# Normalizations merged into the stages that read them, in a six-layer fp32 kernel on one Trainium2 core

## The reference

```python
x = x + 0.5 * moe(_layernorm(x))        # router, 64 experts of 64, the best 8 of each token, a shared expert
x = x + heads(_layernorm(x))            # 16 heads of 8, softmax attention
x = x + 0.5 * moe(_layernorm(x))
x = x + 0.5 * cell(_layernorm(x))       # recurrent: 4 steps (the batch axis), each over all 1024 tokens
x = x + decayed_attention(_layernorm(x))  # its own layernorm, attention, x2; then x2 + mlp(layernorm(x2))
x = x + 0.5 * cell(_layernorm(x))

def _layernorm(x, axis=-1, eps=1e-05):
    m = jnp.mean(x, axis=axis, keepdims=True)
    v = jnp.var(x, axis=axis, keepdims=True)
    return (x - m) / jnp.sqrt(v + eps)
```

## Time and profile before

| | |
|---|---|
| median of 3 runs | 2742.0 us (2739.37 to 2742.69) |
| the profiled execution: time | 2743.51 us |
| the profiled execution: span, first to last instruction | 2741.4 us |
| TensorE busy | 93% |
| VectorE busy | 81% |
| ScalarE busy | 66% |
| GpSimd busy | 45% |
| TensorE's mean granted clock | 0.966 of 2.4 GHz |

### The profile page before, as it was taken

One profiled execution on the slowest core, in us unless ns is written; L12 is line 12 of the kernel. 1 busy time (PEld: TensorE's weight loads), 2 busy tenths in 40 slices (PEclk: granted clock), 3 DMA queues, 4 the chain that ended last, 5 costly groups with the idle time before them and its releaser, 6 DMA issues. The chain is left out here.

```text
span 2741.4 us, 35099 instructions
## 1 busy us (share of the span) xinstructions
PE 2545.0 (93%) x11075; PEld 1905.2 (69%) x11075; DVE 2223.1 (81%) x3277; ACT 1821.2 (66%) x3026; POOL 1231.3 (45%) x1265
## 2 busy tenths in 40 slices
PE   6899999996999999999999997899999998788778
PEld 3688888874666666666666664688888885476556
DVE  6778777776999999999999996777787775567655
ACT  3455555556888888888888884455555555557665
POOL 3466666664323232332323322466666662245401
PEclk9999999998999999999999999999999999888999
DMA  3566666644333333333333321566666640100000
GB/s 85 118 138 145 145 142 135 136 103 164 98 107 99 106 102 97 109 100 104 104 103 101 98 93 34 127 144 138 135 146 145 143 105 8 32 16 8 8 8 31
DMA packets 107385, 271.47 MB, mean 99 GB/s; under 512 B 30784, under 2 KB 35648, under 8 KB 107072
## 3 DMA queue, kind: packets, MB, share of 16 engines
q1 hardware_dynamic: 82192, 235.42, 34.7%
q0 software_dynamic: 24576, 33.62, 4.4%
q10 hardware_dynamic: 432, 0.20, 0.0%
HBM read 258.35 MB, written 10.76 MB: 98 GB/s over the span
## 5 line engine op out<-in xcount | busy, mean ns | idle before, releaser
L614 POOL TENSOR_TENSOR moe_experts_lo<-moe_experts_hidden,moe_experts_hi 128x512 fp32r<-128x512 f32 x512 | 661.1, 1291 | 340.6 <-ACT moe_experts_hi L552 340.4
L895 DVE TENSOR_TENSOR heads_e_lo<-heads_e,heads_e_hi 128x1024 fp32r<-128x1024 f32 x512 | 616.1, 1224 | 25.7
L559 ACT ACTIVATE psum<-psum 128x512 f32<-128x512 f32 x512 | 298.0, 582 | 479.8 <-PE psum L90 479.8
L729 POOL DMA_DIRECT2D heads_left<-heads_parts x512 | 306.5, 612 | 671.3 <-PE psum L783 610.7
L835 ACT ACTIVATE heads_e<-psum 128x1024 f32<-128x1024 f32 x512 | 520.0, 1023 | 108.2 <-PE psum L783 108.2
L586 DVE TENSOR_TENSOR moe_experts_weighted<-moe_spread,psum 128x512 f32<-128x512 f32 x512 | 350.8, 685 | 190.2 <-PE psum L90 186.4
L88 PE MATMUL psum<-heads_e_hi,heads_v_lo 128*128 128x512 f32 x1024 | 429.4, 419 | 18.0 <-DVE heads_u L861 18.0
L88 PE MATMUL psum<-moe_n_hi,moe_w_lo 128*128 128x512 f32 x1024 | 400.8, 391 | 4.2 <-PEq L54 3.9
L89 PE MATMUL psum<-heads_e_lo,heads_v_hi 128*128 128x512 f32 x1024 | 404.2, 395 | 0.0
L90 PE MATMUL psum<-heads_e_hi,heads_v_hi 128*128 128x512 f32 x1024 | 400.9, 391 | 0.0
L89 PE MATMUL psum<-moe_n_lo,moe_w_hi 128*128 128x512 f32 x1024 | 400.2, 391 | 0.0
(11 more groups left out here) (403 smaller groups left out, 4093.8 us busy)
## 6 DMA issues: line engine op xcount, KB each, us to landing
moe_spread<-moe_mask SPq DMA_DIRECT2D x128, 1024.0 KB, 9.8
heads_right<-heads_parts SPq DMA_DIRECT2D x512, 64.0 KB
heads_left<-heads_parts POOLq DMA_DIRECT2D x512, 64.0 KB, 2.5
heads_scale<-heads_inverse_copy SPq DMA_DIRECT2D x64, 512.0 KB, 3.7
moe_experts_raw<-in_gate SPq DMA_DIRECT2D x16, 256.0 KB, 11.7
moe_experts_raw<-in_up SPq DMA_DIRECT2D x16, 256.0 KB, 11.8
moe_experts_raw<-in_down SPq DMA_DIRECT2D x16, 256.0 KB, 11.6
heads_parts<-heads_e_hi SPq DMA_DIRECT2D x16, 256.0 KB, 3.2
```

What stands on the lines that cost most here:

```text
L559: act.activation(psum[:, GATE + p % 2, :], psum[:, GATE + p % 2, :], ACT.Silu).then_inc(silu_ready, 1)
L614: pool.tensor_tensor(lo[:, p, :], hidden[:, p % 2, :], f(hi[:, p, :]), ALU.subtract).then_inc(low_ready, 1)
L729: eng.dma_start(f(tile[row:row + 2 * HEAD, h % 2, :]), parts_dram[dims, order:order + 2, at]).then_inc(loaded[h % 2], 16)
L895: dve.tensor_tensor(e_lo[:, s, :], e[:, s % 4, :], f(e_hi[:, s, :]), ALU.subtract).then_inc(low, 1)
```

## The change

`layernorm` becomes a class `Norm`, whose methods give each engine's part, so that a stage can begin with a normalization and go on with its own work without a barrier. The stages of routing (twice), the cells (twice) and the MLP do so; the heads and the decayed attention keep a stage of their own. In detail:

- The stages wait for chunks instead of the barrier: `wait_low` for a chunk's low part (and with it the high part), `wait_weights` for the early splits, `wait_banks` for all scaled chunks and logarithms, which frees PSUM.
- The variances take two banks (4 and 5) instead of four. The low part of chunk 0 is VectorE's, in all seven.
- The splits of the first experts' weights come behind GpSimd's low parts (`late_splits`).
- Routing: the gate and up products of chunk 0 (`shared(0, 0)`) come right behind `logits(0, 0)`, ahead of the first turn.
- Cells: other banks for the sums (`SUMS`, `OUT`); the high part of the initial cell state is made by VectorE, and the initial state comes ahead of the normalization on its list.
- MLP: the banks of `up` and `down` are permuted so that `up(0, 0)` takes banks 4 to 7.

```diff
+class Norm:
     CENTERED, VARIANCE = 0, 4
-    BANKS = 4
-    RING = 4
-    SCALES = 3
-    VECTOR_LOWS = (2, 5, 7)
+    CENTERS, VARIANCES = 4, 2
+    RING, SCALES = 4, 3
+    VECTOR_LOWS = (0, 2, 5, 7)
...
+    def wait_low(self, eng, c):
+        who = "vector" if c in self.VECTOR_LOWS else "pool"
+        eng.wait_ge(self.low_ready[who], sum((i in self.VECTOR_LOWS) == (c in self.VECTOR_LOWS) for i in range(c + 1)))
+
+    def wait_weights(self, eng, count=None):
+        eng.wait_ge(self.split_low, self.early if count is None else count)
+
+    def wait_banks(self, eng):
+        eng.wait_ge(self.scaled_ready, CHUNKS)
+        eng.wait_ge(self.logs_taken, CHUNKS)
...
+        def variance(c):
+            pe.wait_ge(self.squares_ready, c + 1)
+            after(pe, self.logs_taken, c - self.VARIANCES + 1)
+            pe.matmul(self.psum[:, self.VARIANCE + c % self.VARIANCES, :], self.consts["inv"], self.squares[:, c % 3, :],
+                      start=True, stop=True).then_inc(self.variance_ready, 1)
...
+    def gpsimd(self, pool):
...
+        for i in range(self.early):
+            split(i)
+        for c in range(CHUNKS):
+            if c not in self.VECTOR_LOWS:
+                self.take_low(pool, "pool", c)
+        for i in range(self.early, len(self.splits)):
+            split(i)
...
@@ route_and_share, tensor
                 def logits(c, j):
+                    norm.wait_low(pe, c)
                     after(pe, affinity_ready, c)
...
+                def shared(c, j):
+                    after(pe, added, c - 1)
+                    product(pe, psum[:, GATE + j, :], gate, (n_hi[:, tokens(c)], n_lo[:, tokens(c)]))
+                    product(pe, psum[:, UP + j, :], up, (n_hi[:, tokens(c)], n_lo[:, tokens(c)])).then_inc(up_ready, 1)
+
                 def step(c, j, last):
                     if not last:
                         logits(c + 1, 1 - j)
-                    after(pe, added, c - 1)
-                    product(pe, psum[:, GATE + j, :], gate, (n_hi[:, tokens(c)], n_lo[:, tokens(c)]))
-                    product(pe, psum[:, UP + j, :], up, (n_hi[:, tokens(c)], n_lo[:, tokens(c)])).then_inc(up_ready, 1)
+                    if c > 0:
+                        shared(c, j)
...
+                norm.tensor(pe)
+                norm.wait_weights(pe)
+                pe.wait_ge(norm.scaled_ready, LOGITS + 5)
                 logits(0, 0)
+                pe.wait_ge(norm.log_ready, CHUNKS)
+                shared(0, 0)
+                norm.wait_banks(pe)
                 turn_affinity(0, 0)
...
@@ scalar, vector, gpsimd: each begins with its part of the normalization
+                norm.scalar(act)
                 affinities(0, 0)
...
+                norm.vector(dve)
                 each_chunk(step)
...
+                norm.gpsimd(pool)
                 each_chunk(step)
...
@@ moe_layer
-            layernorm(nc, f"{tag}_norm", psum, consts, x, n_hi[:, :], n_lo[:, :], splits=splits + first_group,
-                      x_dram=x_dram)
+            def normalization(sb, sem):
+                return Norm(sb, sem, f"{tag}_norm", psum, consts, x, n_hi[:, :], n_lo[:, :], splits=splits,
+                            late_splits=first_group, x_dram=x_dram)
...
@@ recurrent_layer
-        OUT = 6
+        start_high = sem("start_high")
+        SUMS = ((6, 7, 4), (5, 0, 1))
+        OUT = 2
...
                 def from_input(t):
                     for half in range(HALVES):
                         at = ds(t * T + half * BANK, BANK)
+                        norm.wait_low(pe, t * HALVES + half)
                         after(pe, gates_ready, t * (3 * HALVES) + (half - 1) * 3)
...
+                norm.tensor(pe)
+                norm.wait_weights(pe)
+                norm.wait_banks(pe)
                 from_input(0)
...
-                act.wait_ge(cell_ready, HALVES)
-                for half in range(HALVES):
-                    act.copy(c_hi[:, half, :], cell[:, half, :]).then_inc(high_ready, 1)
+                norm.scalar(act)
...
                 for half in range(HALVES):
-                    dve.wait_ge(high_ready, half + 1)
+                    dve.wait_ge(cell_ready, half + 1)
+                    dve.tensor_copy(c_hi[:, half, :], cell[:, half, :]).then_inc(start_high, 1)
+                for half in range(HALVES):
+                    dve.wait_ge(start_high, half + 1)
                     dve.tensor_tensor(c_lo[:, half, :], cell[:, half, :], f(c_hi[:, half, :]), ALU.subtract).then_inc(low_ready, 1)
+                norm.vector(dve)
...
@@ mlp_layer
+        def bank(j, m):
+            return psum[:, (1 - j) * W + (m + 2) % W, :]
...
                 def up(c, j):
+                    norm.wait_low(pe, c)
                     after(pe, y_ready, c - 1)
...
+                norm.tensor(pe)
+                norm.wait_weights(pe)
+                pe.wait_ge(norm.log_ready, CHUNKS)
                 up(0, 0)
+                norm.wait_banks(pe)
                 each_chunk(step)
```

More of the change, by code:

```diff
@@ new lines, in take_low, with sync @@
+    def take_low(self, eng, who, c):
+        eng.wait_ge(self.high_ready, c + 1)
+        eng.tensor_tensor(self.n_lo[:, self.chunk(c)], self.normal[:, c % self.RING, :], f(self.n_hi[:, self.chunk(c)]),
+                          ALU.subtract).then_inc(self.low_ready[who], 1)
+    def sync(self, sp):
+        for c, arrived in enumerate(self.x_loaded):
+            sp.dma_start(self.x[:, self.chunk(c)], self.x_dram[:, self.chunk(c)]).then_inc(arrived, 16)
+        for raw, (source, _, _), arrived in zip(self.raws, self.splits, self.raw_loaded):
+            sp.dma_start(raw[:, :], source).then_inc(arrived, 16)
+        for tile, source in self.loads:
+            sp.dma_start(tile, source).then_inc(self.tiles_loaded, 16)
+        if self.copies is not None:
+            for c in range(CHUNKS):
+                self.wait_low(sp, c)
+                for to, part in self.copies:
+                    sp.dma_start(to[:, self.chunk(c)], f((self.n_hi, self.n_lo)[part][:, self.chunk(c)])
+                                 ).then_inc(self.copied[c // HALVES], 16)
+        if self.loads:
+            sp.wait_ge(self.tiles_loaded, 16 * len(self.loads))
@@ new lines, in tensor, with difference @@
+    def tensor(self, pe):
+        def difference(c):
+            if self.x_loaded:
+                pe.wait_ge(self.x_loaded[c], 16)
+            after(pe, self.scaled_ready, c - self.CENTERS + 1)
+            pe.matmul(self.psum[:, self.CENTERED + c % self.CENTERS, :], self.consts["center"], self.x[:, self.chunk(c)],
+                      start=True, stop=True).then_inc(self.difference_ready, 1)
+        def variance(c):
[3 more added lines that the diff above has]
+                      start=True, stop=True).then_inc(self.variance_ready, 1)
+        for c in range(CHUNKS + 1):
+            if c < CHUNKS:
+                difference(c)
+            if c >= 1:
+                variance(c - 1)
@@ new lines, in vector, with scaled, high @@
+    def vector(self, dve):
+        def scaled(c):
+            to, centered = self.normal[:, c % self.RING, :], self.psum[:, self.CENTERED + c % self.CENTERS, :]
+            scale = self.scales[:, c % self.SCALES, :]
+            if c >= self.RING:
+                self.wait_low(dve, c - self.RING)
+            dve.wait_ge(self.scale_ready, c + 1)
+            if self.keep is not None:
+                dve.tensor_tensor(self.keep[:, self.chunk(c)], scale, centered, ALU.mult).then_inc(self.kept_ready, 1)
+                scale = self.both_scales[:, c % self.SCALES, :]
+                dve.wait_ge(self.both_scale_ready, c + 1)
+            dve.tensor_tensor(to, scale, centered, ALU.mult).then_inc(self.scaled_ready, 1)
+            if self.affine is not None:
+                dve.wait_ge(self.scaled_ready, c + 1)
+                dve.tensor_scalar(to, to, self.affine[0], self.affine[1], ALU.mult, ALU.add).then_inc(self.normal_ready, 1)
+        def high(c):
+            dve.wait_ge(self.normal_ready, c + 1)
+            dve.tensor_copy(self.n_hi[:, self.chunk(c)], self.normal[:, c % self.RING, :]).then_inc(self.high_ready, 1)
+        for c in range(CHUNKS + 1):
+            if c < CHUNKS:
+                scaled(c)
+                high(c)
+            if c - 1 in self.VECTOR_LOWS:
+                self.take_low(dve, "vector", c - 1)
+        if self.keep is not None:
+            dve.wait_ge(self.kept_ready, CHUNKS)
@@ L201, in variance @@
-                def variance(c):
-                    pe.wait_ge(squares_ready, c + 1)
-                    after(pe, log_ready if keep is None else both_log_ready, c - BANKS + 1)
-                    pe.matmul(psum[:, VARIANCE + c % BANKS, :], inv, squares[:, c % 3, :], start=True,
-                              stop=True).then_inc(variance_ready, 1)
-                for c in range(CHUNKS + 1):
-                    if c < CHUNKS:
-                        difference(c)
-                    if c >= 1:
```

(2 more changed lines are left out.)

226 lines of the change are left out of this document (103 added, 123 removed).

## The result

| | before | after |
|---|---|---|
| median | 2742.35 us (2739.37 to 2743.34, 4 runs) | 2723.82 us (2723.05 to 2725.68, 4 runs) |
| ratio, 95% interval | | 0.9935 (0.9918 to 0.9952) |
| profiled execution, span | 2741.4 us | 2721.8 us |

The kernel became 18.5 us faster. The prediction was 25.3 us: the sign was right, the size 7 us too large. The prediction's 2716.7 us missed by 7.1 us: the measured median lies 0.2 us inside the range of 2710 to 2724, and 0.8 us above the 2711 to 2723 of rival (a), to which I gave 0.78.

What follows compares the result with a forecast made beforehand. TensorE, busy 93% of 2741.4 us, bounds the kernel, so only its idle gaps can yield. 8.05 + 7.61 - 2.0 + 4.68 + 7.1 - 0.1 = 25.3 us takes the median from 2742.0 to 2716.7; range 2710 to 2724.

Steps and rivals of the forecast that it cites:

- rival (a): Whole kernel: the gain comes as summed, with a time of 2711 to 2723 us; chance 0.78.
- `pick(0)` 3.2 us after the last scale: MoE routing: `pick(0)` follows ScalarE's last scale by about 3.2 us, 6.86 us earlier in the first layer, 6.42 in the second.
- The wait of 1.19 before the first silu: MoE routing: VectorE's idle for `share` before `silu(0)` goes; bounds 0 and 1.19 us, taken in full in each layer.
- The port waits: MoE layers: `pick(0)`'s scalings wait for GpSimd's late splits; bounds 0 and 2.1 us, 1.0 taken per layer, 2.0 together.
- From `silu(0)` on the stage lasts as long as VectorE's list: MoE routing: what arrives earlier at `silu(0)` arrives earlier at the end; gains of 8.05 and 7.61 us.
- The table: MoE layers: ScalarE's Sigmoid table load takes 1.28 us with no drain showing; by the skill page, 1.4 us less won.
- The cells: Both recurrent cells: input products start 2.34 us earlier, TensorE's idle falls from 5.48 to 3.1 us; 4.68 us together.
- "pass on": Cells: the recurrence is a chain and hands on the full 2.34 us; no gain given for the clock.
- rival (b): Whole kernel: cells restart at full clock and splits collide with nothing, 2711.9 us or less; chance 0.08 of below 2711.
- The MLP: MLP stage: the first `y` comes at 2611.5 instead of 2618.59, 7.1 us earlier; 0.8 less if TensorE stays slow.
- the two paths that nearly coincided: MLP, to the first `y`: VectorE's path ends at 2611.4, TensorE's at 2611.5.
- The rest at zero: Other stretches: experts stay at 529 us, later MLP chunks repeat, decay's normalization loses nothing, heads lose 0.1 us.

Runs made afterwards that it cites:

- the run with the constants alone: Against the kernel before, only low part 0 on VectorE and variances in two banks, all stages separate as before: 2738.16 us, ratio 0.9990.

## Why the prediction was 7 us too large

Term by term, from the table of stretches and from the one counted from the first scaled chunk:

- **`pick(0)` 3.2 us after the last scale: right.** ScalarE's last scale ends at 26.99, `pick(0)` starts at 29.90, 2.91 later. From the first scaled chunk it comes 7.14 and 6.71 us earlier, where 6.86 and 6.42 were summed (7.27 and 5.66 by the second traces: in the kernel before, the second layer's normalization differs by 1 us between its two). VectorE's end of the normalization and the turned affinities nearly coincide, as forecast.
- **The wait of 1.19 before the first silu: right.** It is gone.
- **The port waits: the term that was mis-sized.** 1.0 us a layer was taken between 0 and 2.1; it is 2.06, the upper bound, by the same mechanism as in the earlier trace rows: a scaling that meets a GpSimd instruction ends just behind it (33.03 and 33.00; 35.12, after one scaling more, and 34.90). The page of the Trainium skill that said so ("SBUF — State Buffer", Who interferes with whom) is borne out, by 1.13 against 0.17 us. The single row of a wait (1.2 us) was the wrong measure for a list of back-to-back splits, each of which VectorE's next scaling meets anew. 2.1 us in both layers.
- **"From `silu(0)` on the stage lasts as long as VectorE's list": the step that failed.** `shared(0, 0)` left its place in TensorE's queue ahead of the first turned choices, and TensorE had nothing to do until these came: 3.55 us of idle (3.54 in the second layer), half clock for the nine matmuls behind, chunk 0's down product late, and a wait of 1.34 us (1.15) on VectorE. The run with the idle filled takes it away. I credited the move of `shared(0, 0)` with the 1.19 that it won and did not ask what TensorE does in its old place. It cost 1.4 and 1.8 us in the two layers by that run. Up to the second silu it is 1.4 and 1.2; the second layer lost 0.8 us more between there (4.70 us gained) and the experts (3.93), of which filling the idle gave back 0.6. The cause of that part was not isolated.
- **The table: right.** Load and affinity are 0.01 us apart (27.01 + 1.28 = 28.29, then 28.30), and the last scale and the load 0.02 us (26.99, then 27.01). The Trainium skill ("ScalarE: Activation LUTs", What ACT_TABLE_LOAD costs) adds a drain of about 1.38 us to each switch. This trace shows none, on either side of the load.
- **The cells: the start right, the clock not.** TensorE's idle is 3.19 us as forecast, and its first product at 0.77 us in the first cell; but I let 2.34 "pass on" with a restart of the same length as before. From the first product to the first gates the first cell took 7.77 us where it had taken 6.63, the second 6.67 and 6.71. In twelve restarts after 3.19 us of idle (six traces, two cells) the first 18 products came at half clock for 13, 8, 14, 7, 8, 7, 0, 8, 0, 13, 0 and 7 of their steps. So the gain to the first gates was 1.57 us in one trace and 4.3 in another (25.47 us). The changed kernel's own two traces are the first four of these numbers, slow all; the full restarts belong to three kernels with an edit in the MoE layers ahead. My rival (b), a restart at full clock, was real, but not in this kernel, and what decides it was not isolated.
- **The MLP: right, and hidden by what lies ahead.** From the first scaled chunk to the first `y` the kernel before took 28.01 us (36.72 - 8.71) and the changed one 20.81 (30.53 - 9.72): 7.20 us, where 7.1 was summed. VectorE sets it, as one of the two paths that nearly coincided. Low part 0 shows nowhere: VectorE's last low part ends 16.98 us after the first scaled chunk, 16.97 before. The stretch shows 6.19 because the first scaled chunk itself came 9.72 us after the attention's last residual and not 8.71, with less clock over that time (0.59 and 0.64); in the kernel with the MLP's part alone it came after 7.76 us, at 0.72, and the stretch gained 8.1. The windows after, before, and with the MLP's part alone:

```profile
2568.49:2578.21 9.72, 7.85 (x12) 3.31 (x13) 0.01 (x1) 4.32 (x7) 3.71 (x4) 0.59 0.16 55
```

```profile
2581.88:2590.58 8.70, 7.27 (x12) 3.16 (x13) 0.00 (x0) 4.31 (x7) 3.70 (x4) 0.64 0.18 60
```

```profile
2577.05:2584.80 7.75, 6.31 (x12) 2.84 (x13) 0.00 (x0) 4.30 (x7) 3.63 (x4) 0.72 0.22 68
```

- **The rest at zero: wrong in its parts, right in the sum, and that by luck.** +1.2 in the heads, +1.5 in the decay's normalization, +1.8 in the MLP's steady part, -5.4 in the attention. The two constants are not the cause in the first two: the run with the constants alone has the same code there and took 1048.45 and 62.58 us. The clock shows in the attention's windows; for the others it is the likeliest cause, and was not tested.

The edited stretches show 19.4 us where 25.4 were summed. Of the 6.0 that are missing, 1.4 lie ahead of the first silu in the two MoE layers (2.1 of port waits more than were taken, less 0.7 by which the rest came earlier than summed), 2.6 between the first silu and the second, 1.0 from there to the experts, 0.8 in the cells and 0.9 in the MLP; against these stand 0.7 us of an earlier first scaled chunk (15.83 against 16.56).

## What to carry to other kernels

Merging two stages moves work out of the queue places in which it covered something: for each item moved ahead, look at what its engine does in the old place, and whether the clock falls there. A list of GpSimd instructions from SBUF is a wall of short locks for VectorE's scalings and casts; price it at its whole remaining length, and put its pieces behind VectorE's SBUF work, where the scalings here were back at 0.17 and 0.74 us. Ask of each wait for "all" which item each waiting instruction needs: here that was worth 7.6 us of waiting in two cells, and 3.7 us of clock that came with it. And before a difference of a few us is called an effect, cut both traces into stretches and count from an instruction inside the edited stage: here a stretch that no edit touched moved by 8 us, and the MLP's gain was hidden by 1 us ahead of it.

## What the runs showed that I had not expected

- A stretch of 170 us, untouched in all kernels, takes 168.3 to 176.8 us, by how much of it runs at half clock (granted clock 0.91 to 0.86 over the stretch). The kernel before showed its slowest value in both traces, and the changed kernel two values 4.3 us apart.
- After the same idle of 3.19 us TensorE went on at full clock or had half clock for up to 14 matmuls (6 us). After 5.5 to 5.7 us it always began slow, for 6 to 8 matmuls in ten of twelve restarts and for 13 or 14 in two.
- Fifteen useless matmuls in each of two idles of 3.5 us made the two stages shorter, by 3.1 us together.
